# A four-stream decoder kernel: another order of steps in its third and fourth pass, with larger leads of the streams

## Chip, cores, metric

The kernel runs on one core of a Trainium2 chip. The metric is the device time of one execution in microseconds (us). Before the change three runs took 6937.77, 6939.03 and 6943.97 us; the median is 6939.03.

## What is computed

The input is 64 sequences of 256 tokens with 256 features (`x`) and, for each, a context of 77 rows (`ctx_1024`). Two decoder layers of three blocks each are applied, with a layer norm after each block. All attentions have 16 heads of 16 features.

```python
x = _layernorm(x + _L0_attn_ref(x, ...))            # self attention            (A1)
x = _layernorm(x + _L0_xattn_ref(x, ctx, ctx, ...)) # attention to the context  (A2)
x = _layernorm(x + _L0_ffn_ref(x, ...))             # quantised gated MLP       (F)
x = _layernorm(x + _L1_attn_ref(x, ...))            # self attention with rope  (A3)
x = _layernorm(x + _L1_xattn_ref(ctx, x))           # alignment by time warping (D, E)
x = _layernorm(x + _L1_ffn_ref(x, ...))             # gated attention           (A4)

# _L1_xattn_ref: distances of 77 context rows to 256 tokens, cost table by
#   r = d_ij + min(min(up, left), diag), a path traced back, rows of ctx added along it
# _L1_ffn_ref: q is divided by its norm, shifted by query_embedding and scaled; attention;
#   a router (softmax, top 3 of 15) gives one factor per token; out = (h * factor) @ Wp.T + bp
```

## The kernel before

**Passes and streams.** The work is done in four passes over all 64 sequences: A (attention A1), B (A2 and the MLP), C (A3 and the distance table), then the time warping for all sequences at once, then D (path, expansion and A4). Between passes the tokens lie in memory outside the core. In a pass four sequences are in work at a time. They are called streams 0 to 3, each with its own buffers.

**Steps.** A sequence's work in a pass is a chain of named steps, given by `entry(phase, s)`. In C: `xT` (four transposes of the tokens), `q`, `k`, `v` (projections, L704), `rot` (rope: queries on GpSimd, keys on VectorE, L622 to L625), `qT`, `kT` (transposes back, L714), eight `max` steps (L800), two `shift`, four `core` steps (scores L735 and exponentials L938), `pv` (L754) with `take` (L943), `norm` (L823), `oT`, `oproj`, `ln`, `store`, then `xT` of the result, `dist` (L881) and its `store`. In D: `path`, `expand` (L887), `ln`, `xT`, then `q`, `k`, `v`, `rot` (square, a power L996 and scaling on GpSimd, L994 to L1005, with a sum on VectorE, L1063), `qT`, the attention as above, and `oT`, `gate` (L895, and some twenty small operations on VectorE), `oproj`, `ln`, `store`.

A `max` step is the cheap half of the softmax: on TensorE it computes scores in bf16 for two heads into two PSUM banks (L800), and VectorE takes the negated maximum of each row (L1085). `shift` adds it to the queries, so that the exponentials need no further bias.

**Order.** `walk` gives every engine the same list of steps, and each issues its own part of a step in that order. There is no scheduler: an engine waits on semaphores that the other engine's part of a step raises. All steps but `core` write TensorE's results into four PSUM tensors `pj0` to `pj3` in turn (`bank_uses`); TensorE waits before a use until the use four places back has been read out (`wait_bank_free`). The scores have four of their own (`st0` to `st3`), the exponentials three groups.

**Table and lead.** Which stream makes the next step is written out as a string of digits per pass, `ORDER`. Each digit takes the next step of that stream from `turn_of`. `AHEAD[phase][s]` says how many steps at the head of stream s's chain are issued one round early:

```python
late = [load] + chain[cut:] if used < cut else chain[cut:used + 1] + [load] + chain[used + 1:]
return late + chain[:cut]
```

`orders` makes three lists of it: `before` (the lead alone, once), `body` (one round: one sequence of each stream) and `after` (the rest, once). The line of a pass is `before + body * 15 + after`. Loads and stores are issued by the queue SP in the same order.

In the texts below a step is named with its stream: `max3.0` is max step 3 of stream 0. A round is one `body`.

Of the kernel before, what the change touches and what calls it, by code (L numbers as in the profile page):

```python
# [32 lines left out]
D = 256  # L33
S = 256
C = 77
# [130 lines left out]
def entry(phase, s):  # L166

    if phase == "A":
        return before_core("A1", s) + [("fetch", "A", s)] + core("A1", s) + after_core("A1", s) + [("store", "A1", s)]
    if phase == "B":  # L170
        q2, k2, v2, *rest2 = before_core("A2", s)
        return ([k2, v2, ("xT", "B", s), q2] + rest2 + core("A2", s) + after_core("A2", s) + mlp(s)
                + [("store", "F", s)])
    if phase == "C":
        return ([("xT", "C", s)] + before_core("A3", s) + [("fetch", "C", s)] + core("A3", s) + after_core("A3", s)
                + [("store", "A3", s), ("xT", "A3", s), ("dist", "A3", s), ("store", "D", s)])
    return ([("path", "E", s), ("expand", "E", s), ("ln", "E", s), ("xT", "E", s)] + before_core("A4", s) + core("A4", s)
            + after_core("A4", s) + [("store", "A4", s)])


def last_use(phase, s):

    return {"A": ("v", "A1", s), "B": ("norm", "A2", s, 0), "C": ("norm", "A3", s, 0),
            "D": ("expand", "E", s)}[phase]
# [4 lines left out]
          "303133122203303333"),  # L189
    "B": ("303232331303231030120310322321303033312131331212320130213111122013221223021132020133002211"  # L190
          "03230210203310200012131202230101001022032012010101"),
    "C": ("230030000310101100102132100111311001031213121123302212122202011320222310333223332102032012"
          "130233231312023013313322302331002220103232013203101310"),
    "D": ("221203033331301300230103201333220332132301122131023220000213212232121101013312121211310210"
          "13210122310212003000130233102210100013001323323203"),
}

AHEAD = {"A": (8, 4, 1, 0), "B": (21, 21, 30, 32), "C": (13, 6, 7, 1), "D": (28, 33, 6, 14)}


def turn_of(phase, s):

    chain, cut, load = entry(phase, s), AHEAD[phase][s], ("load", phase, s)
    used = chain.index(last_use(phase, s))
    late = [load] + chain[cut:] if used < cut else chain[cut:used + 1] + [load] + chain[used + 1:]
    return late + chain[:cut]


def orders(phase):
# [3 lines left out]
    assert len(body) == sum(len(turn_of(phase, s)) for s in streams)  # L213
    ahead = {step for s in streams for step in entry(phase, s)[:AHEAD[phase][s]]}
    before = [("load", phase, s) for s in streams] + [step for step in body if step in ahead]
# [1256 lines left out]
```

How the kernel before makes its waits and increments, by code:

```python
            @block.tensor  # L418
            def _(pe):
                pe.wait_ge(setup_pool, 1)
                pe.wait_ge(setup_dve, 5)
                pe.matmul(pj[0][:, 0:3], ones[:, 0:P], small[:, 0:3], start=True,
                          stop=True).then_inc(setup_pe, 1)
# [1 line left out]
            @block.scalar  # L425
            def _(act):
                act.wait_ge(consts_loaded, 16 * len(loads))
                act.activation(spx[:, 0, :], temp_sp[:], ACT.Abs).then_inc(setup_act, 1)
                act.wait_ge(setup_act, 1)
                act.activation(spx[:, 1, :], spx[:, 0, :], ACT.Exp, scale=-1.0).then_inc(setup_act, 1)
                act.wait_ge(setup_act, 2)
                act.activation(spx[:, 2, :], spx[:, 1, :], ACT.Ln, bias=1.0).then_inc(setup_act, 1)
# [1 line left out]
            @block.vector  # L434
            def _(dve):
                done = [0]
                def link(ins):
                    done[0] += 1
                    ins.then_inc(setup_dve, 1)
                    dve.wait_ge(setup_dve, done[0])
                dve.wait_ge(setup_pool, 1)
                link(dve.tensor_scalar(wt[:, 0:S], ones[:], 2.0, None, ALU.mult))
                link(dve.tensor_tensor_scan(twice[:], ones[:], wt[:, 0:S], -2.0, ALU.mult, ALU.add))
                dve.wait_ge(consts_loaded, 16 * len(loads))
# [1 line left out]
                    link(dve.tensor_reduce(small[:, i:i + 1], wf[i][:], AX.X, ALU.add,  # L448
                                           apply_absolute_value=True))
                dve.wait_ge(setup_pe, 1)
```

## Time and profile before

| what | value |
|---|---|
| median of three runs | 6939.03 us |
| the profiled execution | 6940.81 us |
| its span, first to last instruction | 6938.8 us |
| mean granted TensorE clock | 0.923 of full |
| pass A, about 44 to 1268 us; pass B, 1268 to 3197 | 1224 us; 1929 us |
| pass C with its setup, 3197 to 4907 | 1710 us, PE busy 1547.3, DVE 1236.7, ACT 976.1, POOL 737.2 |
| time warping, 4907 to 5110 | 203 us |
| pass D, 5110 to 6939 | 1829 us, PE busy 1603.1, DVE 1414.6, ACT 961.4, POOL 1090.4 |
| one projection read out with its bias (DVE, L1053) | 687 ns |
| one shift (DVE, L1092), two to a step | 475 ns |
| key rotation in C (DVE, L622 to L625) | 856 + 750 + 549 + 692 ns |
| one exponential (ACT, L938), four to a core step | 606 ns |
| a token load of 256 KB, issue to landing | 2.9 us |

PE is TensorE's matmuls, PEld its weight loads, DVE is VectorE, ACT ScalarE, POOL GpSimd. Busy time is the union of an engine's instructions, so a busy share near 100% means the engine is hardly ever without one; matmuls are pipelined, and each one's length reaches beyond the start of the next. "Granted clock" is the share of TensorE's full clock that the chip allowed in a stretch.

### The profile page before, as it was taken

The page shows a single profiled execution, that of the slowest core. Times are in us where ns is not written, and L with a number is a line of the kernel's source. Part 1 is how long each engine was busy: PE and PEld are TensorE (multiplying, and loading weights), DVE is VectorE, ACT ScalarE, POOL GpSimd, SP SyncE. Part 2 cuts the span into 40 slices and gives each one's busy share as a digit, 9 for nine tenths or more (in the row PEclk, how much of TensorE's full clock was granted, in tenths as well). Part 3 has the DMA queues.
Part 4 walks back from the last instruction along what each step waited for, and adds up shares of the span by engine and source line. Part 5 has one row for each costly group of instructions (what it writes and reads, how often), then busy time and mean ns, then how long its engine had stood idle before and what let it go on. Part 6 is the DMA issues. An engine that isn't in the chain of part 4 may idle for free. (4 is left out here: it accounts for less than half of the span.)

```text
span 6938.8 us, 142816 instructions
## 1 busy us (share of the span) xinstructions
PE 5833.5 (84%) x54914; PEld 3891.8 (56%) x54914; DVE 5421.7 (78%) x12498; ACT 3827.0 (55%) x7089; POOL 2562.4 (37%) x2572
## 2 busy tenths in 40 slices
PE   6999999688888888886999999999239889898987
PEld 4666666355554545454666666666126666666665
DVE  6888888588888888886777777777668878787786
ACT  5777777345454545453556556556325555555554
POOL 0121121122222222222444543534126566566655
PEclk9999999788888888888999999999669999999999
DMA  1111111100000000000000100100100000000000
GB/s 57 44 41 50 41 43 42 31 20 24 20 24 20 24 20 24 20 18 28 29 28 22 33 28 22 33 26 23 38 19 25 28 18 26 18 28 22 23 28 12
DMA packets 140391, 194.38 MB, mean 28 GB/s; under 512 B 25809, under 2 KB 63697, under 8 KB 139345
## 3 DMA queue, kind: packets, MB, share of 16 engines
q1 hardware_dynamic: 139728, 185.26, 8.6%
q8 instruction: 451, 7.39, 0.5%
q14 instruction: 212, 1.73, 0.1%
HBM read 113.03 MB, written 72.18 MB: 27 GB/s over the span
## 5 line engine op out<-in xcount | busy, mean ns | idle before, releaser
L1085 DVE TENSOR_REDUCE Dmp<-pj 128x2 f32<-128x512 f32 x1024 | 647.2, 684 | 145.0 <-PE pj L800 143.1
L1085 DVE TENSOR_REDUCE Amp<-pj 128x2 f32<-128x512 f32 x1024 | 644.2, 682 | 118.4 <-PE pj L800 118.3
L1085 DVE TENSOR_REDUCE Cmp<-pj 128x2 f32<-128x512 f32 x1024 | 643.3, 684 | 89.9 <-PE pj L800 89.3
L938 ACT ACTIVATE Dpr<-st 128x512 f32<-128x512 f32 x1024 | 528.9, 604 | 276.0 <-PE st L735 275.0
L938 ACT ACTIVATE Apr<-st 128x512 f32<-128x512 f32 x1024 | 528.7, 602 | 274.1 <-PE st L735 272.4
L938 ACT ACTIVATE Cpr<-st 128x512 f32<-128x512 f32 x1024 | 529.5, 606 | 250.6 <-PE st L735 249.2
L1020 POOL TENSOR_SCALAR Bve<-Bmv 128x2 f32<-128x2 f32 x128 | 29.4, 229 | 1345.8 <-DVE Bmv L1152 1345.8
L996 POOL TENSOR_TENSOR Dnrm<-Dnrm,power 128x32 f32<-128x32 f32 x64 | 348.6, 5447 | 162.4 <-DVE Dnrm L1063 162.4
L1020 POOL TENSOR_SCALAR Ave<-Amv 128x2 f32<-128x2 f32 x64 | 14.7, 230 | 1018.7 <-DVE Amv L1152 1018.7
L938 ACT ACTIVATE Bpr<-st 77x512 f32<-77x512 f32 x512 | 262.0, 593 | 191.7 <-PE st L735 191.1
L735 PE MATMUL st<-Dq,Dk 32*128 32x256 f32 x4096 | 346.6, 418 | 22.4 <-DVE Dq L1092 11.8
L735 PE MATMUL st<-Aq,Ak 32*128 32x256 f32 x4096 | 330.3, 397 | 5.5 <-DVE Aq L1092 4.7
L735 PE MATMUL st<-Cq,Ck 32*128 32x256 f32 x4096 | 334.6, 402 | 0.0
L1027 POOL TENSOR_SCALAR Bx<-Bres,Bmv,Brstd 128x256 f32<-128x256 f32 x256 | 315.4, 1241 | 29.5 <-POOL Brstd L1021 29.5
L1027 POOL TENSOR_SCALAR Dx<-Dres,Dmv,Drstd 128x256 f32<-128x256 f32 x256 | 312.8, 1231 | 28.6 <-POOL Drstd L1021 28.6
L1020 POOL TENSOR_SCALAR Cve<-Cmv 128x2 f32<-128x2 f32 x64 | 14.7, 229 | 806.6 <-DVE Cmv L1152 806.6
L961 ACT ACTIVATE Bq<-pj,Bqsc 128x512 f32<-128x512 f32 x256 | 176.5, 690 | 217.1 <-PE pj L853 217.1
L1020 POOL TENSOR_SCALAR Dve<-Dmv 128x2 f32<-128x2 f32 x128 | 29.3, 229 | 700.2 <-DVE Dmv L1152 699.5
L754 PE MATMUL pj<-Dpr,Dv 128*32 128x256 f32 x4096 | 270.4, 408 | 5.1 <-ACT Dpr L938 4.2
L735 PEld LDWEIGHTS st<-Dq,Dk 32*128 32x128 f32 x4096 | 224.3, 195 | 82.6 <-issue 41.6
L887 PE MATMUL pj<-Dctx,Dpath 77*128 77x256 f32 x256 | 72.6, 408 | 234.2 <-DVE Dpath L1124 214.6
L754 PE MATMUL pj<-Cpr,Cv 128*32 128x256 f32 x4096 | 249.1, 384 | 13.1 <-ACT Cpr L938 12.8
(310 smaller groups left out, 16000.7 us busy)
## 6 DMA issues: line engine op xcount, KB each, us to landing
Ax0T<-in_xT SPq DMA_DIRECT2D x64, 256.0 KB, 2.9
Ax<-in_x SPq DMA_DIRECT2D x64, 256.0 KB, 3.3
x_A_scratch<-Ax SPq DMA_DIRECT2D x64, 256.0 KB, 2.0
Bx<-x_A_scratch SPq DMA_DIRECT2D x64, 256.0 KB, 2.9
x_B_scratch<-Bx SPq DMA_DIRECT2D x64, 256.0 KB, 2.0
Cx<-x_B_scratch SPq DMA_DIRECT2D x64, 256.0 KB, 2.9
x_C_scratch<-Cx SPq DMA_DIRECT2D x64, 256.0 KB, 2.1
Dx<-x_C_scratch SPq DMA_DIRECT2D x64, 256.0 KB
```

The costliest lines, as they stand in the source:

```text
L735: ins = pe.matmul(st[bank][0:n, at:at + S], ke[e][s][p0:p0 + 32, c, k:k + n], qe[e][s][p0:p0 + 32, c, :], start=True, stop=True)
L754: ins = pe.matmul(ck.bank(step)[r:r + VW, at:at + S], vv[s][0:n, i, h, :], probs, start=(i == 0), stop=(i == len(tiles_) - 1), skip_group_ ...
L887: ins = pe.matmul(ck.bank(step)[:, t * D:(t + 1) * D], path[s][:, t * P:(t + 1) * P], ctx[s][:], start=True, stop=True)
L938: ck.tell(act.activation(dst, st[bank][0:n, :], ACT.Exp, scale=HD ** -0.5), "probs_ready", step)
L961: ins = act.activation(th[s][:, half, :], ck.bank(use)[:], ACT.Tanh, scale=qsc[s][:, t, 4:5])
L996: link(ck, pool.tensor_tensor(nrm[s][:, 1].rearrange("p t h -> p (t h)"), nrm[s][:, 0].rearrange("p t h -> p (t h)"), power[:], ALU.pow))
L1020: link(ck, pool.tensor_scalar(ve[s][:, :, 0:1], mv[s][:, :, 1:2], EPS, None, ALU.add))
L1027: ins = pool.tensor_scalar(x[s][:, t], res[s][:, t], mv[s][:, t, 0:1], rstd[s][:, t, 0:1], ALU.subtract, ALU.mult)
L1085: ins = dve.tensor_reduce(dst, src, AX.X, ALU.max, negate=True)
```

## The change

Both strings and both leads of C and D are replaced. A and B stay. Nothing else is touched: the steps, their instructions, their number in a round and the buffers are the same.

```diff
-    "C": ("230030000310101100102132100111311001031213121123302212122202011320222310333223332102032012
+    "C": ("331000033303002311021020103223303010330233030013000202213012312101013001231220011133311103
...
-AHEAD = {"A": (8, 4, 1, 0), "B": (21, 21, 30, 32), "C": (13, 6, 7, 1), "D": (28, 33, 6, 14)}
+AHEAD = {"A": (8, 4, 1, 0), "B": (21, 21, 30, 32), "C": (33, 33, 28, 13), "D": (32, 33, 10, 21)}
```

The lead of C grows from 13, 6, 7 and 1 steps to 33, 33, 28 and 13, that of D from 28, 33, 6, 14 to 32, 33, 10, 21. The lists issued once ahead of the rounds become longer (C 31 steps to 111, D 85 to 100, loads included), those behind them shorter (C 113 to 33, D 55 to 40).

VectorE in a round of C, in the stretch with the longest runs of maxima. Cmp is written by a max reduce (L1085), Cv and Cqk by projections, Cq by a shift, Cqr by a rotation. Before:

```order
L1085 TENSOR_REDUCE Cmp<-pj 128x2 x6
L1075 TENSOR_TENSOR Cv<-pj,A_bv 128x32x16
L1092 SCALAR_TENSOR_TENSOR Cq<-pj,mask,Cq 128x256 x2
L1085 TENSOR_REDUCE Cmp<-pj 128x2 x10
L1092 SCALAR_TENSOR_TENSOR Cq<-pj,mask,Cq 128x256 x2
L622 TENSOR_TENSOR Cqr<-Cqk,rope_cos 128x512
L623 TENSOR_TENSOR Ck_3<-Cqk,rope_sin 128x256
L624 TENSOR_TENSOR Ck_3<-Cqk,rope_sin 128x256
L625 TENSOR_TENSOR Cqr<-Cqr,Ck_3 128x512
L1085 TENSOR_REDUCE Cmp<-pj 128x2 x8
```

Now, in the stretch that holds the same rotation of stream 3:

```order
L1053 TENSOR_TENSOR Cqk<-pj,A_bk 128x512
L1092 SCALAR_TENSOR_TENSOR Cq<-pj,mask,Cq 128x256 x2
L1101 RECIPROCAL Crc<-pj 128x16
L1102 TENSOR_TENSOR Cqr<-pj,Crc 128x256
L1085 TENSOR_REDUCE Cmp<-pj 128x2 x8
L1075 TENSOR_TENSOR Cv<-pj,A_bv 128x32x16
L1092 SCALAR_TENSOR_TENSOR Cq<-pj,mask,Cq 128x256 x2
L622 TENSOR_TENSOR Cqr<-Cqk,rope_cos 128x512
L623 TENSOR_TENSOR Ck_3<-Cqk,rope_sin 128x256
L624 TENSOR_TENSOR Ck_3<-Cqk,rope_sin 128x256
L625 TENSOR_TENSOR Cqr<-Cqr,Ck_3 128x512
L1085 TENSOR_REDUCE Cmp<-pj 128x2 x2
```

The runs of ten and (further on) twelve reduces are gone from the round; the longest is now eight, and projections stand between the runs.

TensorE in a round of C, where the projections stand. A_wq, A_wk and A_wv are the projections of the next sequences, A_wo is oproj. Before:

```order
L714 MATMUL pj<-ident,Cx_2 128x128 x4
L704 MATMUL pj<-A_wo,Cqr 128x256 x4
L714 MATMUL pj<-ident,Cx_1 128x128 x4
L714 MATMUL pj<-ident,Cqr 128x128 x8
L704 MATMUL pj<-A_wq,CxT 128x256 x4
L704 MATMUL pj<-A_wk,CxT 128x256 x4
L704 MATMUL pj<-A_wv,CxT 128x256 x4
L800 MATMUL pj<-Ckb,Cqb_0 128x256 x4
L704 MATMUL pj<-A_wq,CxT 128x256 x4
L800 MATMUL pj<-Ckb,Cqb_0 128x256 x4
```

Now:

```order
L714 MATMUL pj<-ident,Cx_2 128x128 x4
L704 MATMUL pj<-A_wo,Cqr 128x256 x4
L811 MATMUL pj<-ident,Cmp 128x128 x2
L714 MATMUL pj<-ident,Cqr 128x128 x4
L704 MATMUL pj<-A_wq,CxT 128x256 x4
L714 MATMUL pj<-ident,Cqr 128x128 x4
L704 MATMUL pj<-A_wk,CxT 128x256 x4
L800 MATMUL pj<-Ckb,Cqb_1 128x256 x4
L735 MATMUL st<-Cq,Ck_0 128x256 x8
L800 MATMUL pj<-Ckb,Cqb_1 128x256 x4
```

The three projections of one stream no longer follow each other; scores (L735) and maxima (L800) of streams further on in their chain come in between, and so over the whole round.

VectorE in a round of D. Dmp is the max reduce, Dres<-pj,Dx the read-out of expand, Dq the shift, Dnrm the sum of squares for POOL, Drc and Dqr the norm step. Before:

```order
L1085 TENSOR_REDUCE Dmp<-pj 128x2 x2
L1148 BN_STATS Dstats<-Dres 128x6 x2
L1152 BN_AGGR Dmv<-Dstats 128x2 x2
L1085 TENSOR_REDUCE Dmp<-pj 128x2 x6
L1092 SCALAR_TENSOR_TENSOR Dq<-pj,mask,Dq 128x256 x2
L1085 TENSOR_REDUCE Dmp<-pj 128x2 x2
L1123 TENSOR_SCALAR Dpath<-twice,Dends 77x256
L1124 SCALAR_TENSOR_TENSOR Dpath<-twice,Dends,Dpath 77x256
L1085 TENSOR_REDUCE Dmp<-pj 128x2 x4
L1101 RECIPROCAL Drc<-pj 128x16
L1102 TENSOR_TENSOR Dqr<-pj,Drc 128x256
L1085 TENSOR_REDUCE Dmp<-pj 128x2 x4
```

Now:

```order
L1085 TENSOR_REDUCE Dmp<-pj 128x2 x4
L1129 TENSOR_TENSOR Dres<-pj,Dx_2 128x512
L1092 SCALAR_TENSOR_TENSOR Dq<-pj,mask,Dq 128x256 x2
L1148 BN_STATS Dstats<-Dres 128x6 x2
L1152 BN_AGGR Dmv<-Dstats 128x2 x2
L1085 TENSOR_REDUCE Dmp<-pj 128x2 x8
L1101 RECIPROCAL Drc<-pj 128x16
L1102 TENSOR_TENSOR Dqr<-pj,Drc 128x256
L1101 RECIPROCAL Drc<-pj 128x16
L1102 TENSOR_TENSOR Dqr<-pj,Drc 128x256
L1092 SCALAR_TENSOR_TENSOR Dq<-pj,mask,Dq 128x256 x2
L1085 TENSOR_REDUCE Dmp<-pj 128x2 x8
```

In D the runs of reduces become longer: over the pass 4 runs of eight before, 33 now.

## Rows read from the trace of the kernel before

**Rows 1.** The page, busy us, share of the span, instructions.

```profile
PE 5833.5 (84%) x54914; PEld 3891.8 (56%) x54914; DVE 5421.7 (78%) x12498; ACT 3827.0 (55%) x7089; POOL 2562.4 (37%) x2572
```

**Rows 2.** Sums over windows from 3202.6 to 4913.8 and from 5116.4 to 6938.8.

```profile
sum 1711.20, PE 1550.97 PEld 1078.27 DVE 1236.50 ACT 976.14 POOL 737.46; mean PE 103.40 PEld 71.88 DVE 82.43 ACT 65.08 POOL 49.16
...
sum 1822.40, PE 1603.13 PEld 1095.01 DVE 1411.19 ACT 961.41 POOL 1090.43; mean PE 123.32 PEld 84.23 DVE 108.55 ACT 73.95 POOL 83.88
```

**Rows 3.** Timeline of SP: start, length, issue; loads of A, C and D.

```profile
166.64 8.03 SPq L658 DMA_DIRECT2D Ax0T<-in_xT  x2
...
240.40 8.03 SPq L658 DMA_DIRECT2D Ax0T<-in_xT  x2
...
3248.75 0.33 SPq L658 DMA_DIRECT2D Cx<-x_B_scratch  x1
...
4717.58 0.33 SPq L658 DMA_DIRECT2D Cx<-x_B_scratch  x1
...
5201.47 0.68 SPq L655 DMA_DIRECT2D Dends<-turns_scratch  x2
...
6744.81 0.71 SPq L655 DMA_DIRECT2D Dends<-turns_scratch  x2
```

**Rows 4.** Windows, rounds of A, C and D: length, busy (count) per engine, clock, DMA.

```profile
400.00:769.00 369.00, 351.77 (x3926) 237.21 (x3926) 299.28 (x600) 274.12 (x501) 67.98 (x80) 1.00 0.14 44
...
3457.90:3563.90 106.00, 97.39 (x929) 67.53 (x929) 77.28 (x149) 61.00 (x112) 46.12 (x52) 0.98 0.09 27
...
3880.10:3984.60 104.50, 95.89 (x930) 66.91 (x929) 77.25 (x150) 61.00 (x112) 46.14 (x53) 1.00 0.09 28
...
5860.90:5971.20 110.30, 99.32 (x928) 67.94 (x923) 87.74 (x245) 59.76 (x113) 68.01 (x57) 0.94 0.08 23
```

**Rows 5.** Windows, two pieces of one C round.

```profile
3984.60:4037.50 52.90, 47.21 (x574) 30.66 (x573) 42.46 (x84) 36.27 (x68) 8.27 (x10) 1.00 0.09 26
...
4037.50:4082.10 44.60, 42.46 (x297) 31.68 (x295) 28.39 (x56) 20.59 (x36) 32.48 (x37) 1.00 0.10 33
```

**Rows 6.** Timeline of PE in that round, in brackets the wait before.

```profile
4010.78 0.63 PE L714 MATMUL pj<-ident,Cqr 128*128 128x128 f32 x4 [0.71 <-DVE Cmp L1085]
...
4070.02 0.66 PE L714 MATMUL pj<-ident,Cqr 128*128 128x128 f32 x4 [0.62 <-POOL Cqr L625]
...
4073.68 1.06 PE L881 MATMUL pj<-CxT,CctxT 128*77 128x256 f32 x4 [0.76 <-POOL Ccsq L1036]
```

**Rows 7.** Timeline of PE in that round, back to back.

```profile
4033.92 0.39 PE L800 MATMUL pj<-Ckb,Cqb 32*128 32x256 bf16 x4
...
4037.65 1.89 PE L704 MATMUL pj<-A_wq,CxT 128*128 128x256 f32 x8
...
4039.38 1.89 PE L704 MATMUL pj<-A_wo,Cqr 128*128 128x256 f32 x8
...
4041.20 1.15 PE L735 MATMUL st<-Cq,Ck 32*128 32x256 f32 x16
...
4042.28 1.93 PE L754 MATMUL pj<-Cpr,Cv 128*32 128x256 f32 x32
```

**Rows 8.** Groups of four C rounds, 3984 to 4403: busy, mean ns, idle before.

```profile
L1085 DVE TENSOR_REDUCE Cmp<-pj 128x2 f32<-128x512 f32 x259 | 162.6, 683 | 21.3 <-PE pj L800 21.2
...
L919 ACT ACTIVATE Ckb<-pj 128x512 bf16<-128x512 f32 x16 | 10.0, 627 | 18.8 <-PE pj L714 18.8
```

**Rows 9.** Timeline of POOL in a D round.

```profile
5813.41 5.44 POOL L996 TENSOR_TENSOR Dnrm<-Dnrm,power 128x32 f32<-128x32 f32 x1 [0.80 <-DVE Dnrm L1063]
```

**Rows 10.** Timeline of PE in that D round.

```profile
5778.19 3.24 PE L704 MATMUL pj<-A_wo,Dqr 128*128 128x256 f32 x8
...
5821.71 0.66 PE L714 MATMUL pj<-ident,Dqr 128*128 128x128 f32 x4 [0.76 <-POOL Dqr L1005]
...
5826.40 3.64 PE L754 MATMUL pj<-Dpr,Dv 128*32 128x256 f32 x32
```

**Rows 11.** Timeline of PE at the end of pass C.

```profile
4902.93 1.12 PE L714 MATMUL pj<-ident,Cx 128*128 128x128 f32 x4 [5.88 <-POOL Cx L1027]
```

More of the change, by code:

```diff
@@ L191 @@
           "03230210203310200012131202230101001022032012010101"),
[L192 to L195, printed above, removed]
+    "C": ("331000033303002311021020103223303010330233030013000202213012312101013001231220011133311103"
+          "131202121211230231122211021222031233221201323302321223"),
+    "D": ("313103031222312013032332201220211213102323222301330313121210122113201111223221303210011301"
+          "02020011000031102303001303210302232300133331002302"),
 }
-AHEAD = {"A": (8, 4, 1, 0), "B": (21, 21, 30, 32), "C": (13, 6, 7, 1), "D": (28, 33, 6, 14)}
+AHEAD = {"A": (8, 4, 1, 0), "B": (21, 21, 30, 32), "C": (33, 33, 28, 13), "D": (32, 33, 10, 21)}
 def turn_of(phase, s):
```

## Prediction, written before the changed kernel was run

> **What bounds the kernel now.** I read the page's busy shares first. TensorE (PE) is busy 84% of 6938.8 us, VectorE (DVE) 78%, ScalarE (ACT) 55%, GpSimd (POOL) 37% [rows 1]. That is an average over stages, so I split the span. The diff touches only the third pass (C) and the fourth (D). From the first load of a pass to its end they are 1711.2 us (3202.6 to 4913.8) and 1822.4 us (5116.4 to 6938.8) [rows 2].
>
> Then one round at a time. A pass is a ramp in, 15 rounds of one fixed order, and a ramp out. The load of stream 0 marks the rounds [rows 3]. Pass C: 3248.75 to 4717.58 is 14 rounds, 104.92 us each. Pass D: 5201.47 to 6744.81 is 14 rounds, 110.24 us each. What is left above 16 rounds is the cost of the ramps: C 1711.2 - 16 x 104.92 = 32.5 us, D 1822.4 - 16 x 110.24 = 58.6 us.
>
> In a C round PE is busy 95.9 of 104.5 us and DVE 77.3. In a D round PE has 99.3 of 110.3, DVE 87.7 and POOL 68.0. An A round is 73.76 us (240.40 - 166.64, [rows 3]); five of them, 369 us, have PE idle for 17.2 us, 4.7%, with DVE at 81% [rows 4]. So the order of A loses about half as much as that of C (8.2%).
>
> Where PE idles in C is seen when one round is cut in pieces [rows 5]: 52.9 us with PE idle 5.7 and DVE busy 80%, then 44.6 us with PE idle 2.1 and DVE at 64%. Most waits in front of PE in the first piece name the reduces of the maxima (L1085), as the first row of [rows 6]. So in one part PE waits for DVE, in the other DVE waits for PE. Only the four pj banks (L800 writes them, L1085 empties them) lie between the two.
>
> **The cost of a step.** Issued back to back at the full clock, from starts in one round [rows 7]: a projection 1.75 us of PE (4039.38 - 4037.65 = 1.73), a core step about 1.08, pv 1.87, a max step 0.33, four transposes 0.44, a shift 0.22, dist 1.75. PE's steps of a C round sum to 91.9 us, of a D round to 89.8. On DVE a max step is two reduces; 259 of them fill 162.6 us [rows 8], so about 1.27 us a step. The other steps' DVE, ACT and POOL costs are the means of the table ahead (projection 0.69, key rotation 2.7, core 2.1 on ACT), less what overlaps. A max step is thus 0.33 on PE against 1.27 on DVE, and a projection 1.75 against 0.69. How these alternate decides who waits.
>
> PE busy / DVE busy for each twelve steps of a C round, by these costs, before: 10/9 6/11 6/6 6/6 8/8 6/5 8/5 10/6 9/3 6/6 9/8 7/8. Changed: 7/6 9/6 9/7 7/4 8/9 8/7 8/6 8/9 9/8 7/7 6/5 6/6. The pair 6/11 and the pair 9/3 are gone.
>
> The Trainium skill (Perfetto Trace Analysis, Identifying the Most-Contended Engine) holds that matmul busy time misjudges how near TensorE is to its limit and that weight-load time is the better sign. In C that is 66.9 of 104.5 us, 64% [rows 4], which would leave far more room than 12.6 us. I keep the 91.9 us floor, since it is made of starts back to back in this trace.
>
> **Part 1, the C round: -80 us.** Two readings.
> (a) By pass A: C reaches A's idle share, 95.8/(1 - 0.047) = 100.5, and loses the slow clock, 0.4 on average: 4 of 14 rounds took 105.9 to 106.0 instead of 104.5, granted 0.98 [rows 4]; that is in the 104.9. Gain 104.9 - 100.5 = 4.4 a round.
> (b) By the order: for every stretch of eight neighbouring steps take the sum of the busiest of PE, DVE and ACT, and average over all starting points. It gives 105.9 for C before (measured 104.9), 74.8 for A (73.8), 105.1 for D (110.2, of which about 5 are the slow clock below). It gives 98.8 for C changed: 7.1 less. Stretches of twelve give 5.2 less, of six 8.1.
> I take (4.4 + 4.4 + 7.1)/3 = 5.3, since (a) is measured: 15 x 5.3 = 80. Bounds: the gain can't exceed the idle and the slow clock, 9 a round (-135). On the other side one new tight pair stands in the changed round: max0.3 comes straight behind kT.3, whose copy L919 takes 0.63 [rows 8], so about 1 us of wait; two old ones go (q to qT of stream 2 with 6.3 us of PE work between, now 10; xT to dist of stream 3 with 2.5, now 3.9), 0.62 and 0.76 [rows 6]. If nothing but this changes it is 0.
>
> **Part 2, the D round: 0.** The same sum gives 106.1 against 105.1: 1.0 worse (stretches of six +0.7, of four -1.4, of sixteen -0.1). The DVE order says why: before, runs of L1085 were mostly of two, with four of eight in the whole pass; now 33 runs of eight, two a round. Against that stand the waits for POOL. Its power (L996) is 5.44 us; the one at 5813 follows directly on another stream's rotation [rows 9], and PE waits 0.76 us for its end [rows 10]. In the changed order rot.1 and rot.0 stand some 30 steps apart, and PE has at least 13.6 us of work from q to qT where it had 11.8.
> The granted clock is 0.95 in D rounds. In the timeline two stretches a round run at the lower level (1.2 GHz): Wo takes 3.24 us where a projection takes 1.89, pv 3.64 where it takes 1.93 [rows 7, 10], together 3.1 us, with scores and maxima beside them. By the granted clock, 5% below full with only 1.2 and 2.4 GHz to choose from, 10% of the round is at 1.2 GHz, 11 us that at 2.4 would be 5.5. I price the two stretches at 5.0. PE had waited several times just before each. Bounds for D: both slow stretches gone and the order not worse, -5 a round (-75); two more and the runs of eight paid in full, +8 (+120). I take 0: the four widths of the sum average 0.05.
> The Trainium skill (TensorE: Matmul & The Clock Gate, A second HAM failure mode: psum-queue depth-cycling) says that a PE which idles briefly and often while it cycles through PSUM banks makes its clock swing, and that the swings cost throughput. The trace agrees for D, and shows C with nearly the same idle share (8.2% against 9.9%) mostly at 1.00. By that rule D would keep its swings for as long as its waits stay.
>
> **Part 3, the ramps: 0.** Before, C issues 31 steps ahead and 113 after; now 111 and 33. In D it is 85 and 55, now 100 and 40. The work is the same, and both tails end in the same chain of one stream: oproj, ln, xT, dist where PE waits 5.88 us for Cx in C [rows 11]. The changed ramp in of C begins with stream 0 nearly alone: four max steps are 5.1 us of DVE with 3.1 of PE beside them. In D qT.1 comes without k.0 and v.0 (3.7 us) ahead of it, at a place where PE waits for POOL already; they fill later gaps instead. I take 0 for both, -15 to +20 together.
>
> **Part 4, the queues: 0.** On SP in C load.1 and load.0 now stand at the head of the round, behind store.1, which waits for ln.1. From oproj.1 PE has about 15 us of work until xT.0 needs the tokens; DVE 1.7, POOL 3.6, the issues 1.5 and a landing of 2.9 (table ahead) are 9.7. So it is covered, by some 5 us less what POOL holds in front. In D load.0 and load.2 are behind stores whose ln is ten steps old. POOL has 46 us of work in a C round, so ln and rot find it free.
>
> **Sum.** 6940.8 (the profiled execution) - 80 + 0 + 0 + 0 = 6861; the median is 1.8 lower than that execution, so 6859, rounded 6860.
>
> **Rivals.**
> R1, the slow clock of D goes as well, since its POOL waits do: -75 + 15 for the runs of eight, 6800. For it: the rotations are apart. Against: DVE waits remain. 0.18.
> R2, C gains only half: the banks couple PE to ACT as well, and DVE waits turn into waits for the exponentials (ACT 61 of 104.5). 15 x 2.5 to 3 = -40, 6900. 0.15.
> R3, the change moves waits without shortening a round: 6926 to 6952. Against it is 6/11 next to 9/3. 0.07.
> R4, slower: D's runs of eight. Four max steps take DVE 5.1 us with 3.2 of PE work beside them (4 x 0.33 and one pv), so PE idles up to 1.9 us twice a round, and each such gap brings a slow stretch of 2.5 us (half of 5.0): 2 x (1.5 + 2.5) = +8 a round, +120, 6980. It decides once D's round grows by more than 5.3 us, C's gain. Against: D has six reduces in a row three times a round already. 0.14.
> The forecast itself 0.46.
>
> **Range and chances.** 6780 to 6940 holds the forecast, R2, most of R1 and part of R3. Under about 0.2%, 14 us, this kernel's time can't be told from no change. Faster: 0.46 + 0.18 + 0.15 = 0.79; same 0.07; slower 0.14.
>
> **What would show it.** A C round of 98 to 101 us, PE idle 4 to 5, DVE waits before Cqk and Cv smaller and no piece of the round with DVE under 70%; granted 1.00 in all C rounds. A D round of 109 to 112 with two slow stretches. Ramps 25 to 50 (C) and 50 to 70 (D). Wrong if C's round stays over 103, if waits for the exponentials replace those for L1085, or if D's round moves by more than 3 us either way.

## The result, and the profile after

The changed kernel takes 6727.3 us (median of 4 runs, 6723.7 to 6732.0), the kernel before in the same session 6941.5 (4 runs, 6937.8 to 6945.8): ratio 0.9694, 95% interval 0.9682 to 0.9707. That is 214 us less by the medians (203 to 221 by the interval), where the prediction said 80 less and ended its range at 6780. The direction was right, the size was not. Of the four runs of d_only below, one took 19843 us at a mean granted clock of 0.543 (0.925 to 0.927 in the others) and is left out.

The page of the changed kernel, in the columns of [rows 1]:

```profile
PE 5683.2 (85%) x54804; PEld 3882.5 (58%) x54914; DVE 5399.0 (80%) x12498; ACT 3825.4 (57%) x7089; POOL 2562.5 (38%) x2572
```

TensorE's (PE's) busy time fell by 150 us although its instructions are the same (x54914 weight loads both times; 110 matmul records are missing after, none of them in C). VectorE, ScalarE and GpSimd hardly moved. Hold on to that line: it is where the prediction broke.

The windows of the third pass (C, 3195.1 to 4755.3) and of the fourth (D, 4958.0 to 6721.6), answering to [rows 2]:

```profile
sum 1560.20, PE 1475.22 PEld 1070.86 DVE 1221.48 ACT 981.44 POOL 733.05; mean PE 1475.22 PEld 1070.86 DVE 1221.48 ACT 981.44 POOL 733.05
...
sum 1763.60, PE 1555.29 PEld 1096.88 DVE 1402.55 ACT 956.44 POOL 1097.33; mean PE 1555.29 PEld 1096.88 DVE 1402.55 ACT 956.44 POOL 1097.33
```

The load marks on SP in C and in D, answering to [rows 3]:

```profile
3283.96 0.92 SPq L658 DMA_DIRECT2D Cx<-x_B_scratch  x2
...
4608.92 0.93 SPq L658 DMA_DIRECT2D Cx<-x_B_scratch  x2
...
5131.82 0.80 SPq L655 DMA_DIRECT2D Dends<-turns_scratch  x2
...
6517.89 0.80 SPq L655 DMA_DIRECT2D Dends<-turns_scratch  x2
```

C: 14 rounds in 1324.96 us, 94.6 each. D: 13 rounds in 1386.07, 106.6 each. All experiments below are read in the same way, as mean rounds by load marks. C's mean moves by up to 0.1 us (94.6 or 94.7) with the stream whose loads are taken. In D single rounds differ by up to 3 us, and the mean moves by up to 0.3 with the choice, so smaller differences in D say nothing.

| us, profiled execution | before | after | difference |
|---|---|---|---|
| C, whole pass | 1711.2 | 1560.2 | -151.0 |
| C, a round | 104.9 | 94.6 | -10.3 |
| C, ramps (pass less 16 rounds) | 32.5 | 46.0 | +13.5 |
| D, whole pass | 1822.4 | 1763.6 | -58.8 |
| D, a round | 110.2 | 106.6 | -3.6 |
| D, ramps | 58.6 | 57.7 | -0.9 |
| the second pass (B), untouched, first load to first load of C | 1925.2 | 1916.8 | -8.4 |
| span | 6938.8 | 6721.6 | -217.2 |

B's 8 us are no part of the change. Of the fourteen profiles of the kernels below, newlead_uneven has B at 1916.8 too and all others at 1923 to 1926, with the old orders and with the new ones, so the 8 us belong to the execution.

One round of C and one of D after, answering to [rows 4]:

```profile
3851.80:3946.30 94.50, 91.06 (x932) 66.45 (x928) 76.40 (x148) 61.30 (x112) 45.79 (x53) 1.00 0.10 30
...
5664.18:5771.60 107.42, 97.34 (x912) 68.32 (x904) 86.53 (x243) 58.37 (x111) 68.43 (x57) 0.94 0.08 24
```

In C, PE idle went from 8.6 to 3.4 us, and PE busy from 95.9 to 91.1, at the granted clock 1.00 in both. Over all rounds the idle time is 8.6 and 3.4 us; its named waits are for VectorE 4.7 and then 2.0, for ScalarE 2.2 and 1.0, for GpSimd 1.3 and 0.4. The idle part is what the prediction could see. The 4.8 us of busy time is what it held to be work.

**What the busy time hid.** Two views show it. First the groups of PE over twelve rounds of C, before (3457.8 to 4717.6) and then after (3378.7 to 4514.4): busy, mean ns of one, idle before.

```profile
L735 PE MATMUL st<-Cq,Ck 32*128 32x256 f32 x3072 | 251.1, 403 | 0.0
L800 PE MATMUL pj<-Ckb,Cqb 32*128 32x256 bf16 x1536 | 148.3, 272 | 48.1 <-DVE Cmp L1085 20.3 <-ACT Cq L911 7.2 <-ACT Ckb L919 6.2
```

```profile
L735 PE MATMUL st<-Cq,Ck 32*128 32x256 f32 x3072 | 236.6, 393 | 0.0
L800 PE MATMUL pj<-Ckb,Cqb 32*128 32x256 bf16 x1536 | 148.4, 270 | 20.0 <-ACT Ckb L919 8.8 <-DVE Cq L1092 6.8 <-DVE Cmp L1085 4.4
```

The same 3072 score matmuls have 14.5 us less busy time and no wait is named in front of them either time. The second view is the timeline before, PE and then ACT, where one such row stands:

```profile
4020.73 0.83 PE L735 MATMUL st<-Cq,Ck 32*128 32x256 f32 x12
4021.48 1.93 PE L754 MATMUL pj<-Cpr,Cv 128*32 128x256 f32 x32
4023.35 1.53 PE L735 MATMUL st<-Cq,Ck 32*128 32x256 f32 x16
4024.80 0.44 PE L811 MATMUL pj<-ident,Cmp 128*128 128x128 f32 x2
```

```profile
4021.63 2.06 ACT L938 ACTIVATE Cpr<-st 128x512 f32<-128x512 f32 x4 [3.52 <-PE st L735]
```

Sixteen score matmuls take 1.45 us from start to start here (4023.35 to 4024.80), and 1.08 in [rows 7]. They begin at 4023.35, while ScalarE is still at the four exponentials of the core step before (until 4023.69), and the four st banks are freed by those one by one. The single matmuls of the row show the wait: those for three of the banks start at 4023.35 and 4023.36, the first one for the last bank at 4023.75, just after the last exponential has ended. PE waits between its own matmuls; since each record reaches beyond the start of the next, the row stays unbroken and counts as busy. So I add up start to start, by the line of the row, over six rounds of C (us a round):

| PE row | before | after | difference |
|---|---|---|---|
| scores L735 | 18.0 | 15.9 | -2.0 |
| maxima L800 | 13.8 | 9.1 | -4.7 |
| shift L811 | 3.6 | 2.6 | -1.1 |
| projections L704 | 29.9 | 29.3 | -0.7 |
| transposes L714, L823 | 17.7 | 15.8 | -1.9 |
| pv L754, dist L881 | 22.1 | 21.9 | -0.2 |

Idle time in front of a row is counted with the row before it. The differences add up to 10.6 us, the gain against these six rounds, of which three ran at 0.98. With the idle time left out, and over six rounds before that all ran at 1.00 (3880.1 to 4507.1), scores go from 17.2 to 15.6 us a round, maxima from 9.8 to 8.0, shift from 2.6 to 2.1, transposes from 14.9 to 14.2, and the rest stays within 0.1: together the busy time that went. Score rows of 14 or more matmuls with over 1.3 us: 21 of 96 before, none of 83 after. Four matmuls of the maxima can be followed by the next row 0.21 us after their start (the shortest tenth), though they are recorded with 0.38.

### The profile page after: what moved, and what is told of

The parts are those of the page before. It is cut to its first block and busy times, and to the rows that moved or that the text cites. A ratio compares the mean times of both kernels' runs of the same rounds, so it can differ in the third digit from the quotient of the medians.

```text
span 6721.6 us, 142690 instructions
## 1 busy us (share of the span) xinstructions
PE 5683.2 (85%) x54804; PEld 3882.5 (58%) x54914; DVE 5399.0 (80%) x12498; ACT 3825.4 (57%) x7089; POOL 2562.5 (38%) x2572
## 5 line engine op out<-in xcount | busy, mean ns | idle before, releaser
L1085 DVE TENSOR_REDUCE Amp<-pj 128x2 f32<-128x512 f32 x1024 | 644.6, 683 | 118.2 <-PE pj L800 118.2
L1085 DVE TENSOR_REDUCE Dmp<-pj 128x2 f32<-128x512 f32 x1024 | 641.1, 684 | 88.4 <-PE pj L800 86.4
L1085 DVE TENSOR_REDUCE Cmp<-pj 128x2 f32<-128x512 f32 x1024 | 642.8, 685 | 82.1 <-PE pj L800 80.9
L1020 POOL TENSOR_SCALAR Bve<-Bmv 128x2 f32<-128x2 f32 x128 | 29.1, 227 | 1339.4 <-DVE Bmv L1152 1339.4
L996 POOL TENSOR_TENSOR Dnrm<-Dnrm,power 128x32 f32<-128x32 f32 x64 | 348.8, 5449 | 196.5 <-DVE Dnrm L1063 196.5
L1020 POOL TENSOR_SCALAR Ave<-Amv 128x2 f32<-128x2 f32 x64 | 14.6, 228 | 1020.2 <-DVE Amv L1152 1020.2
L735 PE MATMUL st<-Aq,Ak 32*128 32x256 f32 x4096 | 330.4, 397 | 5.6 <-DVE Aq L1092 4.7
L735 PE MATMUL st<-Dq,Dk 32*128 32x256 f32 x4096 | 315.7, 398 | 15.8 <-issue 10.0
L735 PE MATMUL st<-Cq,Ck 32*128 32x256 f32 x4096 | 317.2, 394 | 0.7 <-DVE Cq L1092 0.7
L754 PE MATMUL pj<-Dpr,Dv 128*32 128x256 f32 x4096 | 257.5, 393 | 17.0 <-ACT Dpr L938 16.1
L800 PE MATMUL pj<-Dkb,Dqb 32*128 32x256 bf16 x2048 | 200.4, 272 | 77.0 <-DVE Dmp L1085 31.1
L754 PE MATMUL pj<-Cpr,Cv 128*32 128x256 f32 x4096 | 249.0, 384 | 8.7 <-ACT Cpr L938 6.0
L754 PE MATMUL pj<-Apr,Av 128*32 128x256 f32 x4096 | 248.6, 383 | 5.6 <-DVE Amp L1085 2.9
L735 PE MATMUL st<-Bq,Bk 32*77 32x256 f32 x2048 | 200.7, 475 | 57.6 <-issue 34.9
```

The lines of the kernel that those rows point to most:

```text
L735: ins = pe.matmul(st[bank][0:n, at:at + S], ke[e][s][p0:p0 + 32, c, k:k + n], qe[e][s][p0:p0 + 32, c, :], start=True, stop=True)
L754: ins = pe.matmul(ck.bank(step)[r:r + VW, at:at + S], vv[s][0:n, i, h, :], probs, start=(i == 0), stop=(i == len(tiles_) - 1), skip_group_ ...
L800: ins = pe.matmul(ck.bank(step + (i,))[:, first:first + n], qb[e][s][p0:p0 + 32, c, t * P:(t + 1) * P], kb[s][p0:p0 + 32, c, 0:n], start=T ...
L996: link(ck, pool.tensor_tensor(nrm[s][:, 1].rearrange("p t h -> p (t h)"), nrm[s][:, 0].rearrange("p t h -> p (t h)"), power[:], ALU.pow))
L1085: ins = dve.tensor_reduce(dst, src, AX.X, ALU.max, negate=True)
```

## The experiments

**Each pass alone.** c_only has C's order and leads, d_only those of D.

```
 c_only:  ORDER["C"] and AHEAD["C"] of the changed kernel, D as before
 d_only:  ORDER["D"] and AHEAD["D"] of the changed kernel, C as before
```

> The new string and leads for pass C, those of before for D. If the two passes act independently, C takes 1560 us from first load to end (94.6 us a round), D 1822 as before, and the time is 6941 - 151 = 6790 us, with 7 less if pass B again takes less. If the gain of D needs the new C (clock or start of D), the time is the same 6790 and d_only will show the difference. If C gains only together with D, it lies above 6800.

Measured: 6787.6 us, ratio 0.978 (0.9764 to 0.9797); C's round 94.7, D's 110.2.

> The new string and leads for pass D, those of before for C. Independent passes: D takes 1764 us (106.6 a round), C 1711, time 6941 - 59 = 6882 us. The prediction had D at no change (6941 +- 14). If the whole changed kernel's 7 us less in pass B come from the program and not from the execution, they are seen here or in c_only; if from the execution, pass B (load to load 1925 us before, 1918 in the changed kernel) varies with no regard to which pass was changed.

Measured: 6876.4 us (median of three runs, 6874.6 to 6888.7), ratio 0.9918 (0.9901 to 0.9934); C's round 105.2, D's 106.6. By the ratios the two are -153 and -57 us of 6938.3, together -210, where both changes at once give -212 (0.9694). The passes add up. Both parts of the prediction are wrong in themselves: C was given -80, D nothing.

**GpSimd's power in D.** Its 5.4 us per stream (L996, [rows 9]) becomes a multiplication, which leaves the inverse square root out.

```
-  link(ck, pool.tensor_tensor(nrm[s][:, 1]..., nrm[s][:, 0]..., power[:], ALU.pow))
+  link(ck, pool.tensor_tensor(nrm[s][:, 1]..., nrm[s][:, 0]..., power[:], ALU.mult))
```

> The kernel before, with the power of D's rotation on GpSimd (L996, 5.45 us each) replaced by a product (leaves out the inverse root, so queries are wrongly scaled; all shapes and instructions else the same). Theory 1, D before is bound by the GpSimd chain q, rotation, qT (36% of the chain of waits in the stretch around 5815 us): D's round falls from 110.2 to 107 or less. Theory 2, D is bound by how PE and DVE alternate: it falls by less than 1 us. Pass C is the same in both, 104.9.

Measured: 6897.95 us (one run); D's round 108.0, 2.1 less than before.

> The changed kernel with the same power left out. Theory 1, the changed order has taken D off the GpSimd chain: its round stays within 1 us of 106.6, so without the power the two orders differ by 1 us or less. Theory 2, the gain comes from elsewhere: the round stays 3 to 4 us below that of b_nopow.

Measured: 6700.6 us (one run); D's round 105.7, 0.9 less than after. So the power cost D's round 2.1 us in the old order and 0.9 in the new. That is 1.2 of the 3.6 that D gained; without the power the two orders are still 2.3 apart. Both theories' numbers failed: 108.0 is neither 107 or less nor within 1 us of 110.2, and 2.3 is neither 1 or less nor 3 to 4. C's rounds stayed (105.1 and 94.7).

**Is it how evenly the work is spread?** The prediction's reading (b) goes by sums over eight neighbouring steps. After the result I could make it fit C by adding a count of pairs of steps that stand closer than the work between them takes. To test it I searched for orders that are good, or bad, by these two counts: oldlead_even has the old leads and an order that is as even as the changed one, newlead_uneven the new leads and an order as uneven as the one before, even_both in both passes the best orders by the counts.

```
 oldlead_even:    AHEAD["C"] (13, 6, 7, 1),    ORDER["C"] "2000000301320111000133310012..."
 newlead_uneven:  AHEAD["C"] (33, 33, 28, 13), another ORDER["C"]
 even_both:       AHEAD as changed, ORDER["C"] "1303000330331130300102010303...", ORDER["D"] "3310222231323110223213230312..."
```

> The changed kernel, but pass C with the leads of before (13, 6, 7, 1) and a new string of my own. Two counts over the round, with the step costs of the prediction: balance (mean over eight neighbouring steps of the busiest engine's sum) is 98.8, as in the changed C, where before has 105.9; shortfall (for every pair of steps that hand work on, what PE's work between them lacks of the hand-over's length, added up) is 6.7, as in before, where the changed C has 3.1. Theory E (even order and no tight pairs set the round, leads do not): C's round is 94.7 + 3.6 = 98.3 us, 97 to 99.5. Theory L (the larger leads set it): it stays at 103 or more.

Measured: 7254.7 us (one run); C's round 128.9.

> The changed kernel with its own leads in C, but a string that is uneven: balance 105.9 as before the change, shortfall 3.1 as in the changed kernel. Theory E: C's round is 94.7 + 7.1 = 101.8 us, 100 to 104. Theory L: it stays at 94.7, at most 96.

Measured: 7357.5 us (one run); C's round 135.6.

> The changed kernel, both leads kept, with strings for C and D in which the two counts together are as low as I could get them: C balance 96.1 and shortfall 0.6 (changed 98.8 and 3.1), D 99.2 and 1.2 (changed 106.1 and 9.9). Theory E taken at its word: C 94.7 - 2.7 - 2.5 = 89.5, but PE's own work is 91, so 91 to 92.5; D 106.6 - 6.9 - 8.7 = 91, with DVE at 88 and PE at 90 hardly under 97: 97 to 102. Time 6727 - 16 x 3 - 16 x 7 = 6570, 6520 to 6650. Theory L: both rounds stay within 1.5 us, 6700 to 6750.

Measured: 8379.8 us, ratio 1.208 (1.206 to 1.2101); C's round 115.7, D's about 192.

All three are far slower than both kernels. The evenness theory fell, and with it my reading (b) as a way to price an order. That leads alone decide it fell too: the new leads come with 94.7, 115.7 and 135.6. The waits of PE say what the counts had left out. A D stretch of even_both (6000 to 7000): in total, times, longest.

```profile
PE pj L714 <- POOL Dqr L1005: 190.5, 21, 12.1
```

PE stands up to 12 us in front of a transpose, each time for a rotation of D. Such a rotation stands in a queue behind other streams' steps, and not in GpSimd's alone. Before the wait of 11.5 us that ends at 6148.9 GpSimd was idle for 29.6 us in front of the layer norm of another stream (L1020 at 6135.03), and the square of the rotation (L994) came behind it. Before the one of 10.3 us that ends at 6008.7 GpSimd had the square done at 5985.5 and then waited 14.9 us for VectorE's sum (L1063 at 5999.61), which stood behind the gate, maxima and a shift. And busy time again seems to hold waits (window of a round of oldlead_even, columns as in [rows 4]):

```profile
3381.60:3510.70 129.10, 107.43 (x935) 74.16 (x936) 80.82 (x151) 61.82 (x114) 46.73 (x53) 0.92 0.07 22
```

107.4 us busy for a round's matmuls that have 91.1 in the changed kernel. Much of it can be the clock: at a granted 0.92 the slow stretches can have cost up to 10 of the 16 us.

**Is it one kind of work?** The row maxima read half of the keys (the other half is left out), or the exponentials cover half of each tile's columns (the rest of the weights is a constant), in C and D, before and after.

```
+  src = ...[:, :, :, 0:KEYS[att] // 2 if att in ("A3", "A4") else KEYS[att]]      # halfred
+  w = S if att in ("A3", "A4") else QT * S;  act.activation(dst[:, 0:w], st[bank][0:n, 0:w], ...)   # halfexp
```

> Kernel before, but in the third and fourth pass VectorE's row maxima read only half of the keys (the half that is left out is not computed at all). Before this edit the third pass has a round of 104.9 us and the fourth one of 110.2. Theory M (the order before puts TensorE's next reader too close behind VectorE's row maxima, so the round is lost there): the third pass's round falls to 94-97 us, nearly to the 94.7 that the changed order has, and the fourth's by 3 or more. Theory P (the loss sits at GpSimd's or ScalarE's part of a stream's chain, not at the maxima): the third pass's round stays over 102 us, the fourth's over 109.

> Changed kernel with the same edit: the row maxima of the third and fourth pass read only half of the keys. Theory M: the changed order has room for the maxima already, so its rounds (94.7 and 106.6 us) fall by under 1 us, to 94 and 106. Theory P says the same of the third pass, and of the fourth that it falls as much as in the kernel before. Theory E (TensorE is held up by VectorE everywhere, whatever the order): both fall by 3 us or more.

> Kernel before, but ScalarE's exponentials in the third and fourth pass cover only half of each tile's columns (the other half of the weights is a constant set once). Theory M (the maxima on VectorE are the loss): the third pass's round stays within 2 us of 104.9, the fourth's within 2 of 110.2. Theory A (TensorE's reader of the weights stands too close behind the exponentials): the third pass's round falls to 94-98 us and the fourth's to 103-106.

> Changed kernel with the same edit: the exponentials of the third and fourth pass cover half of each tile's columns. Theory M: the third pass's round (94.7 us) moves by under 1 us. Of the fourth (106.6 us), where ScalarE's weights stand in TensorE's longest waits after the change, both theories expect a fall; theory A one of 3 us or more (to 103 or less), theory M one of 1-2 us.

Measured, one run each, rounds in us:

| | total | C before | C after | D before | D after |
|---|---|---|---|---|---|
| unchanged | | 104.9 | 94.7 | 110.2 | 106.6 |
| maxima halved | 6875.1, 6691.1 | 102.9 (-2.1) | 94.4 (-0.3) | 108.1 (-2.1) | 105.1 (-1.5) |
| exponentials halved | 6877.0, 6691.6 | 103.8 (-1.2) | 94.0 (-0.7) | 107.6 (-2.6) | 105.6 (-1.1) |

Theory M wanted 94 to 97 for C before and theory A 94 to 98. Both fell: neither the maxima nor the exponentials alone carry C's loss. Theory P had C's "over 102" right and D's "over 109" wrong; GpSimd's work in C was not tested in this way. Each costs the old order more than the new. In C that makes 1.8 and 0.5 us of the 10.3. In D it makes 0.6 and 1.5, with the 1.2 of the power 3.3 of the 3.6; but these parts can't be added as separate causes, since the clock moved with them. Granted over D's rounds, before and after: 0.944 and 0.957 unchanged, 0.978 and 0.971 with the exponentials halved, 0.956 and 0.968 without the power. The length of a round times what is missing to 1 is the most that its slow stretches can cost. It fell by 3.8 and 1.6 us with the exponentials halved, where the rounds fell by 2.6 and 1.1, and by 1.4 and 1.2 without the power, where they fell by 2.1 and 0.9.

These runs also show the hidden waits. Six rounds of C with halved exponentials (3453.1 to 4076.7), kernel before:

```profile
3453.10:4076.70 623.60, 569.25 (x5570) 397.79 (x5569) 462.99 (x890) 288.51 (x672) 282.51 (x312) 0.99 0.09 28
```

PE has the same 5570 matmul records as in six rounds of the kernel before:

```profile
3457.80:4089.10 631.30, 579.52 (x5570) 403.22 (x5569) 463.71 (x889) 366.01 (x672) 276.86 (x313) 0.99 0.09 27
```

Ten us less "busy" on PE because ScalarE got shorter; at most 1.7 of them are the clock (granted 0.992 in the rows below, 0.994 here). The long score rows go from 21 to 2, and start to start the scores go from 18.0 to 16.7 us a round, the maxima stay (13.6). With halved maxima it is the other way round: maxima 13.8 to 11.5 (with the idle time left out 9.8 to 8.8), and 24 long score rows.

**Is it the queues?** Theory Q: each engine takes its steps in the written order, and a step waits both for its own input and for everything written ahead of it on its engine, other streams' steps included. I walked through the written order step by step with durations from the trace (start to start on PE at the full clock: projection and dist 1.75 us, core 0.96, pv 1.86, four transposes 0.44, shift 0.22, a max step 0.20; the other engines' by their rows), with the waits that the program has. PE's steps of a C round are then about 86 us, and the walk gives rounds of 104.6 and 94.1 for C (measured 104.9 and 94.7) and 108.5 and 105.2 for D (110.2 and 106.6). It has the differences, -10.5 and -3.3, almost exactly, with nothing fitted. It is too low for the three even orders (120, 124 and 111), and has no clock in it.

It was made after those results, so it needed a run of its own. one_rot moves, in C, stream 0's rot and the qT behind it three steps earlier, and in D stream 0's rot six steps later.

```
 PE and POOL, C:  ... shift1.3  dist.1  store.1  rot.0  oT.2  xT.1  qT.0 ...   (step, stream)
             ->   ... rot.0  shift1.3  dist.1  store.1  qT.0  oT.2  xT.1 ...
```

> Changed kernel with one stream's rotation step moved in each pass, nothing else. Third pass: stream 0's rot (and the qT behind it) stands three steps earlier, so that on GpSimd its four operations (5 us) come ahead of stream 1's squares for dist instead of behind them. Fourth pass: stream 0's rot stands six steps later, which brings it nearer to its reader qT. Theory Q (a wait is handed on by the queue that a step stands in; the walk through the written order with the trace's durations): the third pass's round goes from 94.7 to 101.5 us, with a wait of 4 to 5 us of TensorE at dist (in front of the product of the context's features, released by GpSimd's Ccsq) and one of about 2 at Wo; the fourth's from 106.6 to 115.4, with one of 8 to 9 us at the transpose of stream 0's queries. Rival B (the round is set by how the work is spread over TensorE's steps, which two moved steps of no TensorE work hardly change): both rounds within 1 us of the changed kernel's.

Measured: 6999.1 us (one run), 272 slower than the changed kernel from two small moves, and slower than the kernel before; C's round 105.0, D's 114.4. GpSimd's queue in C and PE's row behind it, after that move:

```profile
3400.05 1.27 POOL L622 TENSOR_TENSOR Cqr<-Cqk,rope_cos 128x512 f32<-128x512 f32 x1 [7.43 <-DVE Cqk L1053]
...
3404.23 1.49 POOL L1033 TENSOR_TENSOR Cq<-CxT 128x512 f32<-128x512 f32 x1
...
3407.12 0.76 POOL L1036 TENSOR_TENSOR Ccsq<-Ccsq 128x77 f32<-128x77 f32 x1
```

```profile
3408.14 1.74 PE L881 MATMUL pj<-CxT,CctxT 128*77 128x256 f32 x4 [4.71 <-POOL Ccsq L1036]
3409.68 1.06 PE L881 MATMUL pj<-Cq,neg_half 128*77 128x256 f32 x2
...
3415.19 3.67 PE L704 MATMUL pj<-A_wo,Cqr 128*128 128x256 f32 x8 [2.12 <-ACT Cqr L950]
```

GpSimd sat 7.43 us in front of a rotation whose queries were not there, with the squares, whose input was (the last CxT is written by 3396.7), queued behind it. PE then waited 4.71 us (forecast 4 to 5) and at Wo 2.12 (forecast about 2). Over 14 rounds these two waits are 65.8 and 27.1 us, 4.7 and 1.9 a round, while the next five waits of PE stand as in the changed kernel to 0.1 us in the total (12.5, 10.3, 7.9, 6.2 and 5.1 us). The rest of C's +10.3, 3.7 us, I put down to the clock, which the walk has not: granted 0.95 to 0.98 in these rounds where it was 1.00, with the slow rows just behind the two waits. The single rounds agree: the one granted 0.98 took 103.3 us, those granted 0.97 103.9 to 105.1, those granted 0.95 105.6 to 105.8. In D the round grew by 7.8 (forecast 8.8); PE's waits for the rotation (Dqr L1005) are 6.2 a round in all (forecast 8 to 9 for the one at stream 0's transpose). Rival B (under 1 us in both) is out.

**Does the walk find better orders?** It does not know a round to better than a few us:

> Changed kernel with other orders of the third and fourth pass, leads unchanged, found by a search that walks through the written order with the durations of the trace and adds up TensorE's waits. Theory Q: the third pass's round goes from 94.7 to 93.1 us, the fourth's from 106.6 to 104.3: 62 us less in all, 6665. Rival B (such a walk tells large differences but the remaining waits come from something it lacks, so that an order tuned on it is as likely to lose): both rounds within 1.5 us of the changed kernel's on either side, or slower; total 6700 to 6780. The walk missed the even orders' rounds by 4 to 9 per cent, and halved maxima by 1.4, which speaks for B.

Measured: 6746.9 us, ratio 0.9732 (0.9718 to 0.9745), slower than the changed kernel's 0.9694; C's round 96.9 (forecast 93.1, the walk's own number 92.5), D's 106.2 (forecast 104.3, the walk's 102.9). Rival B was right. Then its durations were fitted to the eleven rounds known so far:

> Changed kernel with other orders of the third and fourth pass, leads unchanged, found by the same walk after its durations were fitted to the eleven rounds measured so far (it now misses the third pass's rounds by -1 to +2 us and the fourth's by under 1). Theory Q, with the walk now good to some 1.5 us: third pass's round 94.7 to 93, fourth's 106.6 to 104.5, in all about 60 us less than the changed kernel (6665). Rival B, what the walk lacks is as large as what it finds: rounds within 1.5 us of the changed kernel's on either side, total 6700 to 6760.

Measured: 6707.6 us, ratio 0.9668 (0.9655 to 0.9681) against the changed kernel's 0.9694 (0.9682 to 0.9707), so faster than both kernels, than the changed one by about 0.27%. Its D round is 105.8, 0.9 less; its C round is 94.6, the same. Of the 60 us that the walk promised, 20 came, inside rival B's 6700 to 6760. So the mechanism behind C's gain is known: one_rot shows waits handed on by a queue, with the place and length of the waits said ahead. That C's 10.3 us are waits of this kind rests on the walk, which gives a new order to some 4 us a round, no better; no run takes single queue waits out of the old order.

## Why the prediction was wrong, point by point

**The step that failed is the bound of Part 1**: "the gain can't exceed the idle and the slow clock, 9 a round (-135)", and reading (a) with it, which held PE's busy 95.8 fixed. C's round gained 10.3. PE's busy time fell by 4.8 us with the same matmuls. The idle time went down by 5.2, close to what (a) gave it (4.4, of which 0.4 was the clock). What the bound held to be work was in part waiting inside unbroken rows of matmuls: for banks that ScalarE still read (scores, 1.7 us less a round), and for VectorE's reduces (maxima, 1.8 less), as the two halvings show.

**The floor under it was counted too high.** "PE's steps of a C round sum to 91.9" has the max step at 0.33, read from one place in [rows 7] where the next row came late, and the core step at 1.08. At their shortest they are followed by the next row after 0.20 and 0.97. 32 x 0.13 and 16 x 0.11 are 5.9 us; the sum is about 86. I had refused the 12.6 us that even 91.9 left, and 86 leaves 19; how much of that an order can get is open beyond the 10.3 that came. The Trainium skill's rule (Perfetto Trace Analysis, Identifying the Most-Contended Engine), which I set aside in favour of that floor, pointed the right way. The trace agrees: weight loads took 66.9 us of a C round before and 66.5 after, while the matmul busy time moved by 4.8. How much of the third of a round that weight loads leave free could be had, no run shows.

**Reading (b), 7.1 a round, was near by accident.** Orders searched for on such sums took 116 to 136 us. It counts how much work lies near a place, not what stands ahead of what in a queue. Taking the mean of (a) and (b) then averaged a reading with a wrong bound and one with no ground; 5.3 was given for 10.3: the rounds of C gained 164 us (16 x 10.28) against the 80 forecast, the largest part of the error, and the longer ramps took 13 of it back.

**Part 2, D at 0, was off by 3.6 a round (58 us).** The sum that gave it (106.1 against 105.1) is the same reading (b). The waits for GpSimd counted more than I gave them (1.2 by the power's runs). But PE's idle time hardly moved: 11.0 us of a D round before, 10.6 after. Its waits for VectorE went from 6.3 to 2.9 and those for GpSimd from 1.6 to 0.4, and those for ScalarE rose from 1.9 to 6.4. D's gain too lies in PE's busy time, 99.3 to 96.0 us a round. The runs of eight reduces did no harm that shows: halving the maxima gives less after (1.5) than before (2.1). The slow clock stayed, as said, but shrank: granted 0.944 before and 0.957 after over the rounds, which can be at most 1.6 of the 3.6. Such rows are still there:

```profile
5335.12 3.47 PE L704 MATMUL pj<-A_wo,Dqr 128*128 128x256 f32 x8
```

How D's 3.6 divide between clock and queues stays open beyond that bound.

**Parts 3 and 4.** The ramps of C grew by 13.5 us and those of D fell by 0.9, together inside -15 to +20. The queues of SP cost nothing that any wait shows.

**The rivals.** R1 had the right size for D (-60 against -58.8), by luck in the main: its slow stretches did not go, and its +15 for the runs of eight did not show. R2, R3 and R4 did not happen. No rival had C's round below 96, though (b)'s own widths reached 8.1. Of "what would show it", C's round (98 to 101) failed from below, and PE idle of 4 to 5 was 3.4, with all rounds of C after at 94.3 to 95.0 and none disturbed. One of its signs of being wrong came: D's round moved by more than 3 us.

## What to carry to other kernels

Before a bound is taken from an engine's busy time, add up the starts: compare the same group of matmuls at its shortest start-to-start with its mean, and count what is above the shortest as waiting, whether or not a wait is named. An order for engines that each take their steps in the written order is priced by walking through it, with every other stream's steps in the queues; sums over neighbouring steps do not do it, and even the walk is good for large differences only, here 10 us in 100 and not 2. One step that is written ahead of its input's arrival on a lightly loaded engine (GpSimd was busy 44% of C's round in one_rot) cost C's round 10.3 of 94.6 us here.

## What the runs showed of the hardware that I had not expected

The matmuls of a C round, the same each time, were recorded with 95.9 us of busy time in the kernel before and 91.1 in the changed one, both at the granted clock of 1.00, and with 107.4 in a bad order at 0.92.

In the changed kernel all rounds of C ran at 1.00, with gaps of at most 0.7 us. In one_rot, with gaps of 4.71 and 2.12 us a round added, they were granted 0.95 to 0.98. The slow rows stand just behind the two gaps: the matmul pair at 3409.68 (L881 x2) took 1.06 us instead of 0.59, and the projection at 3415.19 took 3.67 instead of the 1.89 of [rows 7]. In that order a long wait was dearer than its length, by some 3.7 us on top of 6.6. The kernel before had more idle time in C's rounds (8.6 us) in gaps of under 1 us, and ten of its 14 rounds were granted 1.00; the other four, at 0.98, took 1.4 us longer.
